# Stick-breaking attention: the running row sum is read back from the score tile instead of being made by a matmul of its own

## What is computed

```python
z = einsum('bhid,bhjd->bhij', q, k) / sqrt(64)          # 32 heads of 64
mask = tril(ones((l, l), bool), k=-1)
lom = where(mask, -softplus(z), 0.0)
s = flip(cumsum(flip(lom, -1), -1), -1) - lom            # sum over the keys after j
att = where(mask, exp(log_sigmoid(z) + s), 0.0)
o = einsum('bhij,bhjd->bhid', att, v)
```

## Time and profile before

| | us |
|---|---|
| median of 3 runs | 8464.82 (8420.36 to 8472.5) |
| the profiled execution | 8454.72 |
| its span, slowest core | 8453.2 (cores from 8362.3) |
| busy: PE, ACT, DVE, POOL | 5919.7, 2880.4, 2678.4, 854.2 |
| L636, 1152 matmuls | 559.1 |
| L641, 1152 DVE additions | 673.5 |

### The profile page before, as it was taken

How to read it: one execution, slowest core, us unless ns; L and a number is a source line. 1 busy time by engine, 2 the same in 40 slices (tenths; PEclk the granted TensorE clock), 3 DMA queues, 4 the chain that set the end, 5 groups by cost and what they waited for, 6 DMA issues and landing times.

```text
span 8453.2 us, 79587 instructions; the slowest of 8 cores (8362.3 to 8453.2 us)
## 1 busy us (share of the span) xinstructions
PE 5919.7 (70%) x18740; PEld 1679.7 (20%) x18740; DVE 2678.4 (32%) x4660; ACT 2880.4 (34%) x4306; POOL 854.2 (10%) x1617
## 2 busy tenths in 40 slices
PE   2223668688888888888888856377667767766775
PEld 0001212122222222222222112111212121122212
DVE  7211212222222222222222211166146516623650
ACT  0000334344444444444444500144134405412540
POOL 0001111111000111000010010100110010001001
PEclk9866655666655666666566578688888888878888
DMA  2001547510000000000000034311431161134116
GB/s 76 12 5 10 63 50 88 66 12 7 6 6 7 8 8 8 6 6 6 6 8 1 1 79 98 68 55 55 122 105 55 52 174 55 63 95 124 55 39 172
DMA packets 222099, 408.71 MB, mean 48 GB/s; under 512 B 141576, under 2 KB 144032, under 8 KB 215760
## 3 DMA queue, kind: packets, MB, share of 16 engines
q0 software_dynamic: 200592, 353.00, 20.3%
q1 hardware_dynamic: 20784, 50.47, 2.4%
q10 hardware_dynamic: 272, 0.14, 0.0%
HBM read 451.83 MB, written 85.07 MB: 64 GB/s over the span
## 4 chain that ended last, share of the span: by engine, by line
PE 48%; DMA 18%; DVE 11%; ACT 10%; issue 10%; another core or an unknown queue 2%; DVEq 1%; ACTq 0%; SPq 0%; POOL 0%; POOLq 0%
PE pbq L502 7%; PE zp L624 6%; PE zp L630 6%; DMA cd<-scr_cd 5%; ACT att L557 4%; PE pboA L571 4%; DVE gu L809 4%; PE zp L540 3%; DMA xp<-x 3%; PE pbL L636 3%; PE pboB L571 2%; ACT g L801 2%; DMA wv<-WvT 2%; PE pbL L798 2%
## 5 line engine op out<-in xcount | busy, mean ns | idle before, releaser
L641 DVE TENSOR_TENSOR lsb<-lsb,pbL 1x512 bf16<-1x512 bf16 (+3 forms) x1152 | 673.5, 585 | 1819.5 <-PE pbL L636 1803.1
L598 ACT ACTIVATE texp<-zp 128x1024 bf16<-128x1024 f32 x448 | 458.7, 1024 | 984.3 <-PE zp L540 789.1
L624 PE MATMUL zp<-sp,tri 128*128 128x512 bf16 (+3 forms) x1280 | 653.6, 511 | 5.9 <-ACT sp L610 5.9
L557 ACT ACTIVATE att<-zp 128x1024 bf16<-128x1024 f32 x448 | 458.0, 1022 | 573.1 <-PE zp L630 567.5
L630 PE MATMUL zp<-lsb,ones 1*128 1x512 bf16 (+2 forms) x1152 | 610.8, 530 | 0.0
L571 PE MATMUL pboA<-att,vtok 128*64 128x512 bf16 (+2 forms) x640 | 347.0, 542 | 372.1 <-ACT att L557 302.9
L636 PE MATMUL pbL<-sp,negones 128*1 128x512 bf16 (+3 forms) x1152 | 559.1, 485 | 66.8 <-DVE lsb L641 66.2
L809 DVE TENSOR_TENSOR gu<-g,pbL 128x512 bf16<-128x512 bf16 x704 | 483.7, 687 | 189.2 <-PE pboA L805 62.1
L781 ACT ACTIVATE zg<-zp 128x512 bf16<-128x512 f32 x64 | 38.2, 597 | 1470.8 <-PE zp L778 1470.8
L809 DVE TENSOR_TENSOR gu<-g,zp 128x512 bf16<-128x512 bf16 x704 | 483.8, 687 | 167.4 <-ACT g L801 56.5
L801 ACT ACTIVATE g<-zp 128x512 bf16<-128x512 f32 x704 | 420.3, 597 | 277.1 <-PE zp L795 203.0
(11 more groups left out here) (187 smaller groups left out, 6989.9 us busy)
## 6 DMA issues: line engine op xcount, KB each, us to landing
cd<-scr_cd POOLq DMA_DIRECT2D x256, 512.0 KB, 4.8
cgu<-scr_cgu POOLq DMA_DIRECT2D x136, 704.0 KB, 4.8
scr_cgu<-CguT POOLq DMA_DIRECT2D x32, 704.0 KB, 77.8
x<-x SPq DMA_DIRECT2D x16, 1024.0 KB, 4.9
scr_cd<-CdT POOLq DMA_DIRECT2D x32, 512.0 KB, 75.3
xp<-x SPq DMA_DIRECT2D x64, 256.0 KB, 4.6
out<-op SPq DMA_DIRECT2D x64, 256.0 KB, 3.8
out<-yst POOLq DMA_DIRECT2D x16, 1024.0 KB, 8.6
```

The lines of the kernel that those rows point to most:

```text
L557: Sc.op("ACT", lambda sc, zp=zp: sc.activation(t_att[zp][:], zpair_ap[zp][:], AF.Exp), reads=[pr[(0 if zp == 0 else 6)], pr[(0 if zp == 0 ...
L624: Sc.op("PE", lambda t, zp=zp, h0=h0, c0=c0, pz=pz: t.matmul(zpair_ap[zp][:, h0 + c0:h0 + QT], t_tri[:], t_sp[zp][:, h0 + c0:h0 + QT], sta ...
L641: Sc.op("DVE", lambda v, hs=hs, c0=c0: v.tensor_tensor(t_lsb[hs][:, c0:QT], t_lsb[hs][:, c0:QT], pbank[2][0:1, c0:QT], op=ALU.add), reads= ...
```

## The change

The total that is handed on is no longer made by a matmul. After texp and sp of block jb, DVE copies row 0 of the still untouched scores (z of the block's first key) to a new tile `z0` (1 x 512, float32, one a head). L624 and L630 then add to that row the sum over the whole block and the total before it, so afterwards row 0 holds z0 plus the new total. DVE subtracts `z0` from it and writes `lsb`. The matmul L636 goes; the addition L641 becomes that subtraction, which reads the score banks instead of bank 2. Both are left out for jb = 0, as before.

The scheduler gets one rule more: a read of a PSUM bank by another engine than the one that read it last waits for that last reader. So the copy waits for texp (ACT), and att (ACT) waits for the subtraction (DVE) on either head's bank. L624, which writes the bank, now also waits for the copy.

```diff
 class Res:
-    __slots__ = ("name", "writer", "readers")
+    __slots__ = ("name", "writer", "readers", "psum")
...
     def _events(self, reads, writes, eng=None):
         need = []
         for r in reads:
             need.append(r.writer)
+            if r.psum and r.readers:
+                last = r.readers[-1]
+                if last[0] != eng:
+                    need.append(last)
...
+    for r_ in pr:
+        r_.psum = True
...
+    t_z0 = [sb(f"z0_{i}", [1, QT], F32, s2) for i in range(2)]
...
+                if jb != 0:
+                    for hs in range(2):
+                        pz = (0 if zp == 0 else 6) + hs
+                        h0 = 512 * hs
+                        Sc.op("DVE", lambda v, zp=zp, h0=h0, c0=c0, hs=hs: v.tensor_copy(
+                            t_z0[hs][:, c0:QT], zpair_ap[zp][0:1, h0 + c0:h0 + QT]),
+                            reads=[pr[(0 if zp == 0 else 6) + hs]], writes=[res(f"z0_{hs}")])
                 yield
...
                     if jb != 0:
-                        Sc.op("PE", lambda t, zp=zp, h0=h0, c0=c0, first=(jb == jbmax): t.matmul(
-                            pbank[2][0:1, c0:QT], t_negones[:],
-                            t_sp[zp][:, h0 + c0:h0 + QT],
-                            start=True, stop=True),
-                            reads=[res("negones"), res(f"sp{zp}")], writes=[pr[2]])
-                        Sc.op("DVE", lambda v, hs=hs, c0=c0: v.tensor_tensor(
-                            t_lsb[hs][:, c0:QT], t_lsb[hs][:, c0:QT], pbank[2][0:1, c0:QT], op=ALU.add),
-                            reads=[pr[2], res(f"lsb{hs}")], writes=[res(f"lsb{hs}")])
+                        Sc.op("DVE", lambda v, zp=zp, h0=h0, c0=c0, hs=hs: v.tensor_tensor(
+                            t_lsb[hs][:, c0:QT], zpair_ap[zp][0:1, h0 + c0:h0 + QT],
+                            t_z0[hs][:, c0:QT], op=ALU.subtract),
+                            reads=[pr[(0 if zp == 0 else 6) + hs], res(f"z0_{hs}"), res(f"lsb{hs}")],
+                            writes=[res(f"lsb{hs}")])
```

More of the change, by code:

```diff
@@ L31, with __init__ @@
 class Res:
-    __slots__ = ("name", "writer", "readers")
-    def __init__(self, name):
+    __slots__ = ("name", "writer", "readers", "psum")
+    def __init__(self, name, psum=False):
         self.name = name
@@ L36, in __init__ @@
         self.readers = []
+        self.psum = psum
 class Sched:
@@ L76, in _resolve, with _events @@
         return waits
-    def _events(self, reads, writes):
+    def _events(self, reads, writes, eng=None):
         need = []
@@ L97, in op @@
     def op(self, eng, fn, reads=(), writes=()):
-        waits = self._resolve(eng, self._events(reads, writes))
+        waits = self._resolve(eng, self._events(reads, writes, eng))
         self.count[eng] += 1
```

## The result

The changed kernel takes 8524.38 us (median of 35 runs) where the kernel before, on the same chips, takes 8454.44 (35 runs). The ratio is 1.007, with a 95% interval of 1.0046 to 1.0094: +59 us by the ratio, slower, by less than the 1% named in the prediction. The lowest runs, 8425.25 and 8389.55, lie 36 us apart. The profiled execution is 8508.76 us. That it comes so near to the 8507 forecast is partly chance: in it cores 4 to 7 had a lower mean clock (0.701 against 0.720) and took 8495.4 at the median, cores 0 to 3 took 8427.8.

What follows compares the result with a forecast made beforehand. Without bursts the chain of L540, five matmuls, att and L571 bounds a block; between bursts PE does. 81 + 36 - 70 + 5 = +52 us on 8454.7 gives 8507 us, range 8435 to 8588.

Steps and rivals of the forecast that it cites:

- A: Full attention blocks without projection bursts: att waits for head 1's subtraction, +0.25 us each over 324 blocks, +81 us.
- rival 1: PE's saved time shows: 7829 us if in all blocks, 8290 us in a weaker form; chance 0.12 with the upper clock.
- B: Starts of query tiles without bursts: copies wait behind DVE's clearing of lsb and att, delaying L571; +36 us.
- C: Blocks between projection bursts, six a head pair: both L636 and a hole go, 4.65 us x 15, -70 us.
- D: Where transposes follow the bursts: their DVE copy stands behind subtractions and z0 copies, +0.3 x 15 = +5 us.
- Dearer handovers: Second L630, subtraction, att in full blocks: handovers cost more, 8549 to 8588 us; chance 0.22 with the lower clock.
- The clock rival: Granted clock differs: bursts at the lower level 9083 us (within 0.22), full blocks at the upper level 8118 us (within 0.12).
- my own sign: Prediction wrong if the full-block period is below 5.5 or above 5.9 us, or either stretch's granted clock differs.

Runs made afterwards that it cites:

- the complement: Kernel before, with the new way in all blocks but the six of a head pair followed by projection bursts: 8525.83 us, ratio 1.0127.
- the early clearing: Changed kernel with the clears for the next query tile made in the last block of the tile before: 8438.14 us, ratio 1.0042.
- the later clearing: Changed kernel with the clears of lsb and att behind the first block's z0 copies instead of ahead of them: 8480.32 us, ratio 1.011.
- bursts alone: Kernel before, with the new way only in the six blocks of a head pair followed by projection bursts: 8369.99 us, ratio 0.9938.
- both together: Kernel before, with the new way in the six blocks followed by bursts and both L636 last in blocks without: 8220.72 us, ratio 0.9785.

## Why the prediction came out as it did

*A, full blocks without bursts: right.* Forecast 5.76 us, found 5.77. Each step is in the rows: 0.70 from the matmul to the subtraction (0.71), 0.68 for it, 0.09 to att (0.10). The experiment without att's wait parts the sum into -0.52 and +0.78; I had both. PE's hole I had too small: it is 2.05 us, not 1.5, since it grows by both matmuls that left as well. What I had wrong beside it is the floor of rival 1: I let att start no sooner than the listed end of sp, 0.42 sooner than before, but it started 0.52 sooner, 0.08 ahead of that listed end. ACT's records overlap a little, so an end in them is no hard bound.

*B, starts of query tiles: right in place, somewhat too large.* At tile 3, 3.96 us became 4.68, some +0.7 where I had 0.85. For tile 0 I had +0.55, and the complement shows +0.6; for tile 2 I had +0.8, and of its +2.3 the eight full blocks make 2.1, which leaves 0.2. The cause I named is shown at tile 3 by the early clearing, which takes all of it away. My own remedy, the later clearing, was wrong by the same reasoning: I asked what waits for the copies and not what waits for the subtraction.

*C, blocks between bursts: the term was a little too small where it applied, and applied too often.* The working holds by tile 0 (bursts alone -0.85, forecast -0.85). In tile 1 I had -3.8, and up to the end of the last burst both the changed kernel and the bursts alone are 4.0 shorter (medians, 46.36 to 42.35). By itself the term gave -5.5: with the holes gone, PE often keeps the full clock for some 4 us more behind the last burst, which no row of before could show me. The changed kernel doesn't get that part, as D says. Three of the 15 head pairs wait for DMA in tile 1, where I had counted the gain as well. That wait hides losses too: the three together are 2 us longer on core 1 and 3.6 by the medians of eight cores, in a spread of 10 to 17 us from core to core, where 3 x 2.9 was forecast. So it cost the sum nothing.

*D, transposes: right in kind, its size bound up with the clock.* The wait that I named is in the traces. Behind the last burst, the second transpose waits for DVE's copy of the first, which now stands behind two subtractions and two copies of z0. First the kernel before, then the changed one (core 1):

```profile
2805.60 0.22 PE L518 MATMUL pbq<-idb,vF 128*128 128x128 bf16 x1 [0.90 <-DVE vtok L521]
```

```profile
1828.13 0.22 PE L526 MATMUL pbq<-idb,vF 128*128 128x128 bf16 x1 [2.12 <-DVE vtok L529]
```

That is 1.22 us more, against the 0.98 which the same block saves. I had +0.3 for all of it. The complement shows just that behind the last burst (some 15.8 us for 15.5). The changed kernel also has about 15.5 there, but the bursts alone have 14.2, though both are alike up to that point. In the changed kernel (core 1) the clock falls 5.6 to 6.0 us behind the last burst in eight of 12 head pairs and 2.7 to 3.0 us in four, never as late as the 8.6 to 9.9 of the bursts alone. So the new way in the blocks behind the last burst takes the clock's extra time away again; whether by the longer wait of the transposes or by the two missing matmuls a block, no run parts.

*The sum.* By the traces, 12 x 1.6 + 8.9 + some 3.5 for the first three head pairs is about +31; by all cores +43; by the ratio of the large comparison +59. The forecast was +52. The traces lie some 21 below it: 12 x (2.9 - 1.6) = 16, and 5 in the first three head pairs. Of the 1.3 a head pair, B makes some 0.7 and C and D in tile 1 0.7, against which A is 0.2 larger than forecast. That +52 lies between +43 and +59 is thus partly luck: the 12 to 28 us by which whole executions exceed the +31 are in no row shown here. The stretches at 0.81 of the last section are one candidate, untested; the cause stays open.

*The rivals.* That PE's saving shows everywhere fell with the wait before L579. Dearer handovers fell with the 0.10 from DVE to ACT, though ACT waits for two engines there. The clock rival: 0.50 stayed in the full blocks, as forecast. The bursts kept 1.00 on cores 0 to 3. On cores 4 to 7 four to six of the 12 middle head pairs ran them at 0.81, a level that I had not considered; the 12 took some 2985 us there against 2949. By my own sign, a differing clock in the bursts, that die is a miss. The longer stay of the clock behind the bursts I hadn't priced either. No `tri` matmul stalls in full blocks, since the copies end 1.6 us ahead. PE's busy time fell by 411 us (5919.7 to 5508.7), not the 560 I gave: I had added durations that overlap. DVE's rose by 577 (2678.4 to 3255.0), not 670.

## What to carry to other kernels

A matmul saved is worth what it takes from the path and no more: in the full blocks here 0.52 us of the first one and nothing of the second, and the wait that came with the saving cost 0.78. Before removing an operation, see whether moving it behind the instruction that others wait for gives the same gain free of charge; it did here, and 1.4% with it. And where a new wait is mended by moving work, follow each instruction that stands behind the moved one on its engine, not only the one that stalled.

## What the runs showed of the hardware beyond that

A third spacing of matmuls turned up in stretches, in the changed kernel's profiled execution on one die. Its core 4 at one burst, and the window of that query tile:

```profile
3524.03 4.36 PE L510 MATMUL pbq<-xnF,wk 128*128 128x512 bf16 x16
```

```profile
3509.00:3576.00 67.00, 60.10 (x214) 20.40 (x212) 24.76 (x50) 21.23 (x29) 11.60 (x22) 0.75 0.11 11
```

16 matmuls in 4.36 us are 0.27 each, where a burst in the full state took 3.63, 0.23 each; the granted clock over that burst is 0.81, and the tile took 67 us in the place of 58, at a mean clock of 0.75. In the profiled executions of the kernel before, of the complement and of the changed kernel with the early clearing, no burst of the 12 middle head pairs ran so; with the bursts alone, some did on all eight cores. With one such execution a kernel, what brings it on isn't shown. The Trainium skill (TensorE: Matmul & The Clock Gate, "Seeing it yourself") tells of a peak-current limit at 13/16 of the clock for a die of which three cores run dense matmuls; 3.63 x 16/13 is 4.47, an estimate by that page which the row, at 4.36, nearly meets.

Two sums into different banks start 0.38 us apart (2868.17 and 2868.55 in the rows of both together, at the lower clock), where the `tri` and `ones` matmuls of the same width, into the two score banks, follow each other at 0.54; why isn't shown. And with the sums last, core 0 had a few full blocks in which the clock rose without any burst: rows of its timeline, 0.32 apart.

```profile
2866.44 0.39 PE L642 MATMUL zp<-sp,tri 128*128 128x512 bf16 x1
2866.76 0.39 PE L648 MATMUL zp<-lsb,ones 1*128 1x512 bf16 x1
```

That block took 4.51 us (2865.04 to 2869.55). Such stretches are short and rare, and I found them only where the sums stand last: of the 800 us or more that tile 3 takes a core behind its first 17 us (13 head pairs), the granted clock was 1.00 for 0 to 31 us in the four kernels with that order, on all cores but one, and for none in the kernel before, the changed one and the one without att's wait. What makes one block reach the upper level and not the next stays open.
